# A gated cross-attention block with routed experts on one core: input statistics one group ahead, scaling on VectorE, and another order at the start

## What is computed

```python
h  = layer_norm(_layernorm(x), g_x, b_x)
c  = layer_norm(ctx_768, g_c, b_c)
q, k, v = h @ Wq, c @ Wk, c @ Wv                 # 16 heads, within each of 128 sequences
a  = softmax(q k^T / 8) v
x2 = x + tanh(g_xattn) * (a @ Wo)
n2 = _layernorm(x2)
e  = argmax(n2 @ router_w);  p = max softmax(n2 @ router_w)
out = x2 + tanh(g_ffn) * p * (gelu(n2 @ w1[e] + b1[e]) @ w2[e] + b2[e])
```

## Time and profile before

| | |
|---|---|
| median of three runs | 895.61 us (891.29 to 896.56) |
| the profiled execution | 898.15 us, of which its span is 896.4 |
| busy in the span: TensorE, VectorE, ScalarE, GpSimd | 767.8, 576.8, 509.3, 632.4 us |
| mean granted clock of TensorE | 0.927 of full speed |

### The profile page before, as it was taken

How to read it: one execution, slowest core, us unless ns; L and a number is a source line. 1 busy time by engine, 2 the same in 40 slices (tenths; PEclk the granted TensorE clock), 3 DMA queues, 4 the chain that set the end, 5 groups by cost and what they waited for, 6 DMA issues and landing times. The chain is left out here.

```text
span 896.4 us, 34833 instructions
## 1 busy us (share of the span) xinstructions
PE 767.8 (86%) x12659; PEld 701.6 (78%) x12660; DVE 576.8 (64%) x1565; ACT 509.3 (57%) x986; POOL 632.4 (71%) x1230
## 2 busy tenths in 40 slices
PE   0899998999999999999999999999999974488882
PEld 0788888888888888888888888888888864488881
DVE  3256666777666767676767676767666762476772
ACT  2555666666665656666666565656556631365661
POOL 6666677777777777777777777777777655277774
PEclk9989999999999999999999999999999965598996
DMA  4651001110000000000000101010100000365540
GB/s 113 187 143 26 15 23 31 37 34 28 28 28 28 28 28 28 28 28 28 28 28 28 32 24 34 24 31 28 30 18 15 31 19 15 105 173 145 140 117 7
DMA packets 50526, 43.90 MB, mean 49 GB/s; under 512 B 14632, under 2 KB 46026, under 8 KB 50474
## 3 DMA queue, kind: packets, MB, share of 16 engines
q1 hardware_dynamic: 43898, 30.53, 12.8%
q0 software_dynamic: 5632, 12.67, 4.0%
q10 hardware_dynamic: 944, 0.01, 0.1%
HBM read 28.55 MB, written 15.68 MB: 49 GB/s over the span
## 5 line engine op out<-in xcount | busy, mean ns | idle before, releaser
L582 ACT ACTIVATE OT_h<-psO 128x1024 fp32r<-128x1024 f32 x64 | 65.7, 1026 | 127.2 <-PE psO L770 127.2
L474 POOL TENSOR_TENSOR probs<-probs,row_inv 128x1024 f32<-128x1024 f32 x64 | 121.8, 1904 | 7.8 <-DVE row_inv L1005 7.1
L985 DVE TENSOR_REDUCE row_max<-psS 128x16 f32<-128x1024 f32 x64 | 78.3, 1224 | 66.1 <-PE psS L748 66.1
L1000 DVE TENSOR_REDUCE row_sum<-probs 128x16 f32<-128x1024 f32 x64 | 77.7, 1215 | 66.6 <-ACT probs L595 66.6
L573 ACT ACTIVATE KT<-psJ 128x512 f32<-128x512 f32 x128 | 76.3, 596 | 54.8 <-PE psJ L691 49.3
L1013 DVE TENSOR_TENSOR OT_l<-psO,OT_h 128x1024 fp32r<-128x1024 f32 x64 | 78.1, 1221 | 26.6 <-ACT OT_h L582 26.5
L573 ACT ACTIVATE QT<-psJ 128x512 f32<-128x512 f32 x128 | 75.8, 594 | 20.9 <-PE psJ L691 18.0
L689 PE MATMUL psJ<-CT_h,Wk_h 96*128 96x256 f32 x256 | 85.4, 334 | 2.0 <-ACT QT L573 1.9
L770 PE MATMUL psO<-PTs,V 64*64 64x64 f32 x4096 | 85.6, 240 | 1.5 <-ACT PTs L589 0.8
L689 PE MATMUL psJ<-XT_h,Wq_h 128*128 128x256 f32 x256 | 81.6, 319 | 5.9 <-POOL CT_l L491 5.9
L573 ACT ACTIVATE V<-psJ 128x512 f32<-128x512 f32 x128 | 76.1, 595 | 15.0 <-PE psJ L691 11.8
(11 more groups left out here) (172 smaller groups left out, 2302.9 us busy)
## 6 DMA issues: line engine op xcount, KB each, us to landing
V<-rows_by_expert SPq DMA_DIRECT2D x40, 129.0 KB
QT<-rows_by_expert SPq DMA_DIRECT2D x40, 129.0 KB, 2.3
x_in<-in_x_dram SPq DMA_DIRECT2D x32, 128.0 KB, 2.2
x_res<-in_x_dram SPq DMA_DIRECT2D x32, 128.0 KB, 2.4
c_in<-in_ctx_dram SPq DMA_DIRECT2D x32, 96.0 KB, 2.3
rows_by_expert<-pad_row SPq DMA_DIRECT2D x1, 1806.0 KB, 12.7
w_sb<-in_L_ffn_w_dram SPq DMA_DIRECT2D x1, 1792.0 KB, 8.1
rows_by_expert<-rows,place_i POOLq DMA_INDIRECT x64, 2.7
```

The source lines that it names most:

```text
L474: pool.tensor_tensor(pr, pr, row_inv[:, p.k % 2, :].unsqueeze(2).to_broadcast([P, 16, SEQ]), ALU.mult).then_inc(s_norm, 1)
L985: dve.tensor_reduce(row_max[:, :], psS[:, :].rearrange("p (n k) -> p n k", k=SEQ), AX.X, ALU.max).then_inc(s_max, 1)
L1000: dve.tensor_reduce(row_sum[:, :], pr, AX.X, ALU.add).then_inc(s_sum, 1)
```

## The change

Statistics of the input are taken three groups ahead instead of two. Roots of that group and of the x2 rows are still computed together by GpSimd, at the same place; but the scalings `norm_in` and `norm_x2` are VectorE's now. `norm_in` stands behind `stats_in` at the head of VectorE's even step and uses the roots of the group before's round; `norm_x2` stands in the odd step behind `scores_max` and uses this round's. Further:

- TensorE's odd step has the input transposes behind job 9 and the value sums; the even step has the first probability transposes in front of job 2 and the router behind job 3.
- VectorE's odd step has `prep` in front of `scores_sub`; its even step has `means_in` behind `scores_sub`, and `sums` in front of `values_low`.
- ScalarE's odd step has `expo` in front of job 10, and both halves of `probs_out` in front of `attn_out`.
- At the start VectorE computes the first roots itself (`first_roots`), and `low` parts and inputs alternate in another order; GpSimd splits a group before it computes the next one's roots. TensorE executes 12 products of the identity with itself in front of the first transposes and 8 behind them (`spin`), and the scores of the first step come in front of jobs 10 and 11 of group 0.

```diff
@@ -401,22 +401,21 @@
 
             def roots(p):
 
-                g_in, g_x2 = p.group(-2), p.group(2)
+                g_in, g_x2 = p.group(-3), p.group(2)
                 if g_in is None and g_x2 is None:
                     return
-                n = NEWT * (p.g + 2)
+                n = NEWT * (p.g + 3)
                 if g_in is not None:
-                    pool.wait_ge(s_agg, 4 * (p.g + 3))
+                    pool.wait_ge(s_agg, 4 * (p.g + 4))
                 if g_x2 is not None:
                     pool.wait_ge(s_agg2, 2 * (p.g - 1))
                 pool.tensor_tensor(nw[:, :], mv[:, :, 1], var_mul[:, :], ALU.mult).then_inc(s_newton, 1)
                 pool.wait_ge(s_newton, n + 1)
                 pool.tensor_tensor(nw[:, :], nw[:, :], var_add[:, :], ALU.add).then_inc(s_newton, 1)
 
-                if not (p.fixed and p.g < -1):
-                    if not (p.fixed and p.g + 1 >= GROUPS):
-                        pool.wait_ge(s_z, 4 * (p.g + 2))
-                if not (p.fixed and not 0 <= p.g - 3 < GROUPS):
+                if not (p.fixed and p.g + 2 < 0):
+                    pool.wait_ge(s_z, 4 * (p.g + 3) if not p.fixed else 4 * min(p.g + 3, GROUPS))
+                if not (p.fixed and p.g - 3 < 0):
                     pool.wait_ge(s_n2, 2 * (p.g - 2))
                 pool.wait_ge(s_newton, n + 2)
                 pool.tensor_tensor(nh[:, :], nw[:, :], halves[:, :], ALU.mult).then_inc(s_newton, 1)
...
-            def norm_in(p):
-                pool.wait_ge(s_newton, NEWT * (p.g + 3))
-                if not (p.fixed and p.g < -1):
-                    pool.wait_ge(s_prep, p.g + 2)
-                pool.sem_inc(s_scaled, 1)
-                for t in range(2):
-                    pool.tensor_scalar(zx[:, t, :], x_in[:, par, t, :], rstd[:, t:t + 1], shift[:, t:t + 1],
-                                       ALU.mult, ALU.subtract).then_inc(s_z, 1)
-                for t in range(2):
-                    pool.tensor_scalar(zc[:, t, :], c_in[:, par, t, :], rstd[:, 2 + t:3 + t], shift[:, 2 + t:3 + t],
-                                       ALU.mult, ALU.subtract).then_inc(s_z, 1)
...
-            def norm_x2(p):
-                pool.wait_ge(s_newton, NEWT * (p.g + 3))
-                pool.sem_inc(s_scaled, 1)
-                for t in range(2):
-                    pool.tensor_scalar(rows[:, par, t, D:2 * D], rows[:, par, t, 0:D], rstd[:, 4 + t:5 + t],
-                                       shift[:, 4 + t:5 + t], ALU.mult, ALU.subtract).then_inc(s_n2, 1)
...
@@ -517,17 +486,12 @@
                     normalise(p)
                 else:
                     roots(p)
-                    norm_in(p)
                     normalise(p)
-                    norm_x2(p)
-
+
+            split_in(Plan(-1, 0))
             roots(Plan(-1, 0))
-            norm_in(Plan(-1, 0))
-            split_in(Plan(-1, 0))
+            split_in(Plan(-1, 2))
             roots(Plan(-1, 2))
-            norm_in(Plan(-1, 2))
-
-            split_in(Plan(-1, 2))
             run(pool, step)
...
@@ -619,11 +583,11 @@
                     values_high(p)
                     job(p, 9)
                     norm_T(p)
+                    expo(p)
                     job(p, 10)
-                    expo(p)
                     probs_out(p, 0)
+                    probs_out(p, 1)
                     attn_out(p)
-                    probs_out(p, 1)
                     job(p, 11)
...
@@ -852,9 +816,9 @@
                 if p.odd:
                     scores(p)
                     job(p, 8)
+                    job(p, 9)
+                    value_sums(p)
                     prep(p)
-                    value_sums(p)
-                    job(p, 9)
                     probs_T(p, 0)
                     job(p, 10)
                     post_b(p)
@@ -863,14 +827,18 @@
                     probs_T(p, 1)
                 else:
                     scores(p)
+                    if p.fixed and p.s == 0:
+                        job(Plan(-1, 2), 10)
+                        job(Plan(-1, 2), 11)
+                        pe.wait_ge(s_wl, 4)
                     value_sums(p)
                     job(p, 0)
                     job(p, 1)
                     post_a(p)
+                    probs_T(p, 0)
                     job(p, 2)
+                    job(p, 3)
                     router(p)
-                    job(p, 3)
-                    probs_T(p, 0)
                     job(p, 4)
                     job(p, 5)
                     probs_T(p, 1)
@@ -878,16 +846,21 @@
                     job(p, 6)
                     job(p, 7)
 
+            def spin(n):
+                for _ in range(n):
+                    pe.matmul(psO[:, 0:P], ident[:, :], ident[:, :], start=True, stop=True)
+
             pe.wait_ge(s_cc, 2)
+            spin(12)
             prep(Plan(-1, 0))
-            for n in range(12):
+            spin(8)
+            for n in range(10):
                 if n in (0, 4, 5):
 
                     pe.wait_ge(s_wl, (0, 4, 5).index(n) + 1)
-                if n == 6:
+                if n == 7:
                     prep(Plan(-1, 2))
                 job(Plan(-1, 2), n)
-            pe.wait_ge(s_wl, 4)
             run(pe, step)
...
             def stats_in(p):
 
-                if p.group(-2) is None:
-                    return
-                par = p.par()
-                dve.wait_ge(s_in[par], 32 * p.uses(-2))
-                if not (p.fixed and p.g < -1):
-
-                    dve.wait_ge(s_agg, 4 * (p.g + 2))
+                if p.group(-3) is None:
+                    return
+                par = p.par(-3)
+                dve.wait_ge(s_in[par], 32 * p.uses(-3))
+                if not (p.fixed and p.g < -2):
+
...
+            def norm_in(p):
+
+                if p.group(-2) is None:
+                    return
+                par = p.par()
+                dve.wait_ge(s_newton, NEWT * (p.g + 3))
+                if not (p.fixed and p.g < -1):
+
+                    dve.wait_ge(s_prep, p.g + 2)
+                for t in range(2):
+                    dve.tensor_scalar(zx[:, t, :], x_in[:, par, t, :], rstd[:, t:t + 1], shift[:, t:t + 1],
+                                      ALU.mult, ALU.subtract).then_inc(s_z, 1)
+                for t in range(2):
+                    dve.tensor_scalar(zc[:, t, :], c_in[:, par, t, :], rstd[:, 2 + t:3 + t], shift[:, 2 + t:3 + t],
+                                      ALU.mult, ALU.subtract).then_inc(s_z, 1)
+
+            def norm_x2(p):
+
+                if p.group(2) is None:
+                    return
+                par = p.par()
+                dve.wait_ge(s_newton, NEWT * (p.g + 4))
+                for t in range(2):
+                    dve.tensor_scalar(rows[:, par, t, D:2 * D], rows[:, par, t, 0:D], rstd[:, 4 + t:5 + t],
+                                      shift[:, 4 + t:5 + t], ALU.mult, ALU.subtract).then_inc(s_n2, 1)
...
-                dve.wait_ge(s_newton, NEWT * (p.g + 2))
+                dve.wait_ge(s_newton, NEWT * (p.g + 3))
...
@@ -1096,21 +1095,23 @@
             def step(p):
                 if p.odd:
                     scores_max(p)
+                    norm_x2(p)
+                    prep(p)
                     scores_sub(p)
-                    prep(p)
                     weight(p)
                     values_low(p)
                     sums(p)
                 else:
                     stats_in(p)
-                    means_in(p)
+                    norm_in(p)
                     scores_max(p)
                     scores_sub(p)
+                    means_in(p)
                     residual(p)
                     means_x2(p)
                     route(p)
+                    sums(p)
                     values_low(p)
-                    sums(p)
                     places(p)
...
-            for g in (-2, -1):
-                q = Plan(-1, 2 * (g + 2))
-                stats_in(q)
-                means_in(q)
-                for i in (0, 1) if g == -2 else (2, 3):
-                    lo, hi, raw = lows[i]
-                    dve.wait_ge(s_wh, i + 1)
-                    dve.tensor_tensor(lo, raw, hi, ALU.subtract).then_inc(s_wl, 1)
-                if g == -2:
-                    dve.wait_ge(s_small, N_SMALL)
-                prep(q)
+            def first_roots():
+
+                dve.wait_ge(s_agg, 4)
+                dve.tensor_tensor(nw[:, :], mv[:, :, 1], var_mul[:, :], ALU.mult).then_inc(s_newton, 1)
+                dve.wait_ge(s_newton, 1)
+                dve.tensor_tensor(nw[:, :], nw[:, :], var_add[:, :], ALU.add).then_inc(s_newton, 1)
+                dve.wait_ge(s_newton, 2)
+                dve.tensor_tensor(nh[:, :], nw[:, :], halves[:, :], ALU.mult).then_inc(s_newton, 1)
+                dve.tensor_scalar(rstd[:, :].bitcast(I32), nw[:, :].bitcast(I32), -0.5, RSQRT_SEED,
+                                  ALU.mult, ALU.add).then_inc(s_newton, 1)
...
+                for _ in range(NEWTON):
```

(44 more changed lines are left out.)

9 lines of the change are left out of this document (2 added, 7 removed).

## The result

The changed kernel is slower: 924.85 us, median of 4 runs (918.80 to 928.35), against 894.33 for the kernel before on the same chip (4 runs). The ratio is 1.0336, with a 95% interval of 1.0267 to 1.0406. The prediction was 837 us, range 824 to 869.

The account below looks back on a forecast made before the run. TensorE plus its wait for `zc`, with clock falls behind it, was taken to bound the loop. Savings 52.1 + 3.2 + 1 + 2.7 = 59.0 from 898.15 profiled gave 839.1; timed runs 2.5 less: 837 us, range 824 to 869.

Parts of the forecast that it names:

- The wait for `zc` goes: Loop: TensorE's wait of 1.48 us per group for GpSimd's last scaled context block disappears.
- 20.2 us per group: Loop of 27 groups: 20.0 us of TensorE work plus 0.2 of new waits (bounds 20.0 and 21.2); 52.1 us less.
- What speaks against it: Loop: VectorE scalings and GpSimd might hold each other up, normalising of 1.89 us the first scaling; taken as nothing.
- The falls go with the waits: Loop: clock falls of 1.71 us each, seen behind waits for `zc`, vanish with those waits.
- The engines block one another: Rival, loop: six scalings each meet a GpSimd operation, VectorE loses about 6 us per group; 936 us, chance 0.05.
- The wait moves: Rival, loop: TensorE waits 0.8 us more at probability transposes or output products, half the falls stay; 869 us, chance 0.20.
- The falls stay: Rival, loop: clock falls remain though the waits go, 20.5 us more; 857 us, chance 0.10.
- The start: Start: first job 3.4 us earlier, then lost again; first maxima near 37.0; 1 us less (bounds 4 less, 3 more).
- The end: Behind 715 us: shorter scalings of the x2 rows cut TensorE's waits; 2.7 us less (bounds 1 and 6).
- The size of VectorE's operations: Loop: six new VectorE operations at 0.25 us each, 1.5 per group (bounds 0.9 and 3.2), 16.9 busy of 20.

Follow-up runs that it names:

- the scaling moved: Changed kernel with VectorE's input scaling (`norm_in`) behind the even step's subtraction instead of at its head: 837.8 us, 0.939 (third job); 0.948 and 0.951 in the earlier jobs.
- the odd step's order taken back: The kernel with the scaling moved, plus TensorE's and VectorE's odd-step orders as before the change: 824.7 us, ratio 0.925 to the kernel before.
- the kernel without the hold-up: Changed kernel with VectorE's input scaling behind the even step's subtraction: 837.8 us, ratio 0.939 to the kernel before.
- third job: Last runs, on one chip without the gap: changed kernel 923.3 us (1.036), scaling moved 837.8 (0.939), odd step also back 824.7 (0.925).
- the kernel with the old orders: Changed kernel with step orders of TensorE, ScalarE and VectorE as before, scaling still at the even step's head: 923.9 us, ratio 0.965 to the kernel before.

## Why the prediction was wrong, point by point

**The wait for `zc` goes.** Right, in both ways of doing it.

**20.2 us per group.** The sum was right for a kernel without the hold-up: with the scaling moved the groups are 20.30 us apart and the kernel takes 837.8 us. The waits that it named are there: `OT_l` late at the output products, 0.37 us in the median (named 0.1), and a V job 0.2 us longer in front of the x2 transposes (0.99 against 0.78 before; named 0.15). With the odd step's order taken back the first one goes and the second stays, and 19.94 us remain, close to the 20.0 of TensorE's own work.

**What speaks against it.** Here is the step that failed. The prediction named the mechanism (a normalising of 1.89 us could hold the first scaling at the head of the even step) and then took "nothing in the middle, since the even step of VectorE is early by several us". It isn't. Several us lie only between the subtraction, at 3.8 in its count, and the odd scores at 9.9; but two others want VectorE's results earlier: the router wants the x2 rows at 5.8 us, which came near 4.6 in the same count, 1.2 us of slack; and the exponential stands in ScalarE's queue in front of the evictions of jobs 2 and 3. A lateness of 2.1 us is more than either has.

In the sum this step put the hold-up at 0, and the falls with it. Measured on the first chip, a group takes 23.42 us: the 20.30 of the kernel without the hold-up (third job, whose chip is of the same kind), 1.41 at the router and job 4, and 46.1 / 27 = 1.71 of falls. 27 x (23.42 - 20.2) = 87 us of the miss of 88 lie there. The rest nearly cancels: the groups ahead of the loop were to be 4.2 us shorter and were 0.7 longer, and the end gained 3.8 more than forecast.

SBUF — State Buffer in the Trainium skill (section "Who interferes with whom") says that the one that comes second stands still until the first is through. The trace agrees that a VectorE scaling stands still until GpSimd's normalising is through: 2.36 us against 0.34 where GpSimd is idle. That the scaling was the second is not shown: the profile has it begin 0.3 to 0.8 us ahead of the normalising, and the profile's own page calls spans on GpSimd rough. The prediction had read this rule, and its sum needed it.

**The falls go with the waits.** As a link this holds as far as the runs go: on the two chips without the gap, the changed kernel with its wait of 0.8 to 1.2 us at the router in 25 of 27 groups had 24 and 21 falls, and the two kernels without that wait had none. On the chips with the gap the kernel before (1.4 to 1.5 us) had 9, the kernel with the old orders (18.4 / 26 = 0.7 us at the router, about 0.9 in 11 groups) none. So a wait of 0.9 us alone doesn't make a fall. The error was in the other direction: shorter waits than before (about 1 us at the router instead of 1.5) brought twice the falls. Why a wait of 1.5 us brings a fall in 11 of 27 groups (9 on another chip) and one of 0.8 to 1.2 in 24 was not tried, and stays open. With it 27 of the 35 us are explained by where they are seen, not by why they come.

**The rivals.** "The engines block one another" was the right mechanism with the wrong price and the wrong threshold: six blocked operations and 6 us per group were assumed to be needed, 2.6 at the least. One blocked operation per group, 2.1 us, was enough, because its lateness became a wait of TensorE, and a fall came with the wait. It had a chance of 0.05. The count that spoke against it, that all places but one lie 1 us or more apart, missed one more: with the scaling moved, the scaling of the x2 rows meets the other normalising of the group (556 ns in the mean against 357 in the changed kernel). That costs nothing, since `xf` behind it waits 1.18 us for TensorE anyway. "The wait moves" named other places (the probability transposes, the output products) and 0.8 us; the wait moved to the router and job 4. "The falls stay" expected them without a wait; they came with one.

**The start.** Right in nearly all: VectorE, GpSimd and TensorE at the start:

```profile
9.01 0.56 DVE L955 TENSOR_SCALAR zc<-c_in,rstd,shift 128x96 f32<-128x96 f32 x2
...
36.09 0.60 DVE L952 TENSOR_SCALAR zx<-x_in,rstd,shift 128x128 f32<-128x128 f32 x2 [1.94 <-POOL shift L436]
...
37.08 1.22 DVE L984 TENSOR_REDUCE row_max<-psS 128x16 f32<-128x1024 f32 x1
```

```profile
13.87 2.65 POOL L456 TENSOR_TENSOR XT_h<-xf,zero 128x256 fp32r<-128x256 f32 x1 [10.66 <-DVE cf L977]
...
17.85 0.72 POOL L460 TENSOR_TENSOR CT_l<-cf,CT_h 96x256 fp32r<-96x256 f32 x1
...
35.85 0.20 POOL L436 TENSOR_TENSOR shift<-mv,rstd 128x6 f32<-128x6 f32 x1
```

```profile
3.17 5.49 PE L851 MATMUL psO<-ident 128*128 128x128 f32 x24 [3.17 <-POOL before L397]
...
18.71 0.55 PE L653 MATMUL psJ<-XT_h,Wq_h 128*128 128x256 f32 x1 [6.63 <-POOL CT_l L460]
```

Scaling done at 9.57 (predicted 9.5), split at 18.57 (18.5) with the disturbed `XT_h` at 2.65 us, first job at 18.71 and at low clock in spite of the idle products (granted clock 0.50 from 18 to 22 us), roots ready at 36.05 (36.2), first maxima at 37.08 (37.0). The first job is 3.3 us earlier, and that is lost again behind `norm_in`, as said. In the third job the first maxima begin at 36.61, and with the scaling moved at 34.05: its place cost 2.6 us here too.

**The end.** 2.7 us were forecast, 6.5 were found behind the loop. The wait for the x2 rows gave what was said, 8.1 us before and 5.2 after; the other 3.6 were not taken apart. **The size of VectorE's operations:** 0.34 us instead of 0.25 each. It is not what failed: with the scaling moved VectorE is busy 469.07 / 27 = 17.4 us per group, against 16.9 in the forecast.

## What to carry to other kernels

Before work is moved from GpSimd to VectorE, look at what GpSimd does at the very place where it will run: a scaling of 0.34 us cost 1.4 us in the mean there, and 2.8 us of kernel time per group. An operation at the head of an in-order queue has the slack of the earliest consumer of anything behind it, so list them all, those that wait through a third engine's queue too. And a new wait of TensorE of 1 us is priced with the fall of the clock behind it, which cost as much again on the two chips where it was there.

## What the runs showed of the hardware

- The same two kernels compare at 1.034 and 1.036 on two chips and at 0.975 on another. The kernel before took 893 to 894 us on the first kind and 957 to 962 on the second, where its second stage and last groups take 250 us instead of 201, and the value sums follow the start of its even scores after 2.2 us instead of 1.0. A change whose gain is a wait can change sign with such a gap.
- VectorE's scaling of 128 x 128 fp32 elements from SBUF took 339 ns beside an idle GpSimd and 2.3 to 2.8 us where it was held until the end of a GpSimd operation of 1.9 us. A small one (128 x 2, `rows<-inv,tanhs`) took 0.74 us at 303.37 in the changed kernel, beside GpSimd's `XT_l` of 0.74 us, and 0.25 in the mean in the kernel before.
- GpSimd's own split was held as well: `XT_h` 2.65 us beside two subtractions on VectorE, 0.61 in the loop.
